# Second attention's beginning: values copied by GpSimd, q's transfers on two queues in both parts, q arranged ahead, second x turned a job later

## The reference, cut to what matters

```python
def _L1_attn_ref(x, Wq, bq, Wk, bk, Wv, bv, Wo, bo):
    # W = 32, H = 16 heads, G = 2 groups of keys and values, D = 16, R = H // G = 8
    q = (xp @ Wq + bq).reshape(B, Lp, H, D).transpose(0, 2, 1, 3)
    k = (xp @ Wk + bk).reshape(B, Lp, G, D).transpose(0, 2, 1, 3)
    v = (xp @ Wv + bv).reshape(B, Lp, G, D).transpose(0, 2, 1, 3)
    starts = jnp.arange(num_windows) * (W // 2)
    idx = starts[:, None] + jnp.arange(W)
    qw, kw, vw = q[:, :, idx, :], k[:, :, idx, :], v[:, :, idx, :]
    qg = qw.reshape(B, R, G, num_windows, W, D)
    scores = jnp.einsum('brgnqd,bgnkd->brgnqk', qg, kw) * scale
    attn = jax.nn.softmax(scores, axis=-1)
    og = jnp.einsum('brgnqk,bgnkd->brgnqd', attn, vw)
    o = og.reshape(B, H, num_windows, W, D).transpose(0, 2, 3, 1, 4).reshape(B, num_windows * W, H * D)
    return o[:, :L, :] @ Wo + bo
```

## Time and profile before

| | |
|---|---|
| median of 3 runs | 1158.51 us (1154.85 to 1162.67) |
| the profiled execution's own time | 1155.04 us |
| its span in the trace | 1153.2 us |
| TensorE busy | 1114.8 us, 97% of the span |
| VectorE busy | 743.3 us, 64% |
| ScalarE busy | 525.1 us, 46% |
| GpSimd busy | 252.7 us, 22% |

### The profile page before, as it was taken

How to read it: one execution, slowest core, us unless ns; L and a number is a source line. 1 busy time by engine, 2 the same in 40 slices (tenths; PEclk the granted TensorE clock), 3 DMA queues, 4 the chain that set the end, 5 groups by cost and what they waited for, 6 DMA issues and landing times. The chain is left out here.

```text
span 1153.2 us, 20280 instructions
## 1 busy us (share of the span) xinstructions
PE 1114.8 (97%) x7188; PEld 960.1 (83%) x7188; DVE 743.3 (64%) x1582; ACT 525.1 (46%) x978; POOL 252.7 (22%) x290
## 2 busy tenths in 40 slices
PE   8999999999999999999999999899998889899997
PEld 7997988989989989988988888775555778788897
DVE  6665665665665665665665677755554767686556
ACT  5675344344344344344344354555552466644322
POOL 1112021021021021111111131323332556323211
PEclk9999999999999999999999999799998969999999
DMA  4001001001001001001000000853333324000001
GB/s 156 11 1 37 11 1 38 9 0 36 9 0 36 9 0 36 9 0 36 9 0 1 1 1 4 318 123 97 98 102 96 87 77 147 1 1 1 19 19 38
DMA packets 27979, 48.28 MB, mean 42 GB/s; under 512 B 4780, under 2 KB 18060, under 8 KB 26764
## 3 DMA queue, kind: packets, MB, share of 16 engines
q1 hardware_dynamic: 23980, 37.62, 10.2%
q0 software_dynamic: 3456, 9.44, 3.1%
q10 hardware_dynamic: 480, 0.40, 0.1%
HBM read 35.65 MB, written 9.44 MB: 39 GB/s over the span
## 5 line engine op out<-in xcount | busy, mean ns | idle before, releaser
L880 POOL TENSOR_TENSOR linear_out_row<-linear_out_row,lin_sq 128x512 f32<-128x512 f32 x62 | 89.9, 1450 | 538.3 <-ACT lin_sq L745 536.0
L43 PE MATMUL lin_bank<-keep_xT_hi,lin_w_hi 128*128 128x512 f32 x382 | 154.2, 404 | 0.0
L44 PE MATMUL lin_bank<-keep_xT_lo,lin_w_hi 128*128 128x512 f32 x382 | 151.1, 395 | 0.0
L45 PE MATMUL lin_bank<-keep_xT_hi,lin_w_lo 128*128 128x512 f32 x382 | 150.8, 395 | 0.0
L825 DVE TENSOR_TENSOR lin_st<-lin_bank,lin_mask 128x512 f32<-128x512 f32 x64 | 44.0, 691 | 160.9 <-PE lin_bank L622 160.9
L741 ACT ACTIVATE lin_o<-lin_bank 128x512 f32<-128x512 f32 x64 | 38.3, 599 | 187.7 <-PE lin_bank L653 187.7
L649 PE MATMUL lin_bank<-lin_st,lin_v 128*128 128x128 f32 x512 | 93.8, 275 | 0.0
L653 PE MATMUL lin_bank<-lin_qd,lin_state 128*128 128x128 f32 x448 | 87.2, 276 | 0.0
L45 PEld LDWEIGHTS lin_bank<-keep_xT_hi,lin_w_lo 128*128 128x128 f32 x382 | 71.8, 188 | 17.5
L44 PEld LDWEIGHTS lin_bank<-keep_xT_lo,lin_w_hi 128*128 128x128 f32 x382 | 72.0, 189 | 14.6
L43 PEld LDWEIGHTS lin_bank<-keep_xT_hi,lin_w_hi 128*128 128x128 f32 x382 | 72.0, 188 | 14.6
(11 more groups left out here) (417 smaller groups left out, 2843.2 us busy)
## 6 DMA issues: line engine op xcount, KB each, us to landing
lin_raw<-in_wp SPq DMA_DIRECT2D x7, 1024.0 KB, 4.7
experts_up_expert_up<-in_wgu SPq DMA_DIRECT2D x16, 352.0 KB, 7.3
sorted_y<-shared_loaded SPq DMA_DIRECT2D x40, 128.0 KB, 1.7
linear_out_row<-in_wdn SPq DMA_DIRECT2D x4, 704.0 KB
lin_raw_out<-in_wop SPq DMA_DIRECT2D x8, 256.0 KB, 2.6
tokens_x<-linear_out_row SPq DMA_DIRECT2D x4, 512.0 KB, 10.3
linear_out_row<-in_ffn_up SPq DMA_DIRECT2D x2, 1024.0 KB, 5.8
tail_q<-tail_qT SPq DMA_DIRECT2D x28, 64.0 KB, 2.0
```

The costliest lines, as they stand in the source:

```text
L43: nc.tensor.matmul(out, lh, rh, start=first, stop=False, skip_group_check=skip)
L44: nc.tensor.matmul(out, lh, rl, start=False, stop=False, skip_group_check=skip)
L45: return nc.tensor.matmul(out, ll, rh, start=False, stop=last, skip_group_check=skip)
L880: pool.tensor_tensor(part, part, sq[:, a, :], ALU.add).then_inc(squares_sb, 1)
```

## The change

Five things are changed in `window_attention`:

1. `duplicate(0)` leaves ScalarE. GpSimd does its four copies (L2526 of the changed kernel), after the gathers of the two groups `used` and ahead of b's two `pool_scale`; ahead of the copies it waits until the gathers of the last three tiles have landed, and behind them until the copies are done. TensorE's `turn_v` waits for the new count.
2. q's transfers of part (0, 1) are shared like those of (0, 0): four on SyncE, four on ScalarE. Batch 1's stay on SyncE.
3. `arrange(0, 1)` is taken from VectorE (job 0's place) and `arrange(1, 1)` from ScalarE's loop (i = 2); both are done by ScalarE ahead of the loop, behind `arrange(1, 0)`.
4. ScalarE loads its table of the exponential ahead of `arrange(0, 0)` instead of behind it.
5. TensorE turns b's x at i = 2 instead of i = 1.

```diff
--- before.py
+++ after.py
@@ -2496,13 +2496,13 @@
                             at = b * 2 * GD + half * GD + g * WD
                             sp.dma_start(k2[at:at + WD, half, g, :], kvT[g * WD:(g + 1) * WD, b, half * STEP:half * STEP + WPAIRS * WIN]).then_inc(k_moved[b], DMA)
                     for rr in range(RR):
-                        move_q(sp, b, rr, (0, 1) if b == rr == 0 else range(4))
+                        move_q(sp, b, rr, range(4) if b else (0, 1))
                 sp.wait_ge(taken, TT)
                 for n in range(BATCH * RR):
                     sp.wait_ge(q_moved[n], 8 * DMA)
                 for b in range(BATCH):
                     sp.wait_ge(k_moved[b], 4 * DMA)
-                sp.wait_ge(vdup_sb, BATCH)
+                sp.wait_ge(vdup_sb, 2 * WG + 1)
                 fetched.load(sp, w["ffn_up"], w["ffn_down"])
 
             @block.gpsimd
@@ -2517,6 +2517,14 @@
                 (a, b), (c0, c1) = used, rest
                 for n, t in enumerate(ORDER):
                     if n == BATCH * USED_TILES:
+                        for t_ahead in ORDER[n - AHEAD:n]:
+                            pool.wait_ge(arrived[t_ahead], 2 * DMA)
+                        pool.wait_ge(kv_sb, 2)
+                        for half in range(2):
+                            v = kvT[GD:2 * GD, 0, half * STEP:half * STEP + WPAIRS * WIN].rearrange("p (m k) -> p m k", k=WIN)
+                            for g in range(WG):
+                                pool.tensor_copy(vdup[GD:2 * GD, :, half, g, :], v).then_inc(vdup_sb, 1)
+                        pool.wait_ge(vdup_sb, 2 * WG)
                         b.pool_scale(pool, chain, "y")
                         b.pool_scale(pool, chain, "x")
                     if n >= RING:
@@ -2613,8 +2621,6 @@
                         dve.wait_ge(before.added, 1)
                         for half in range(2):
                             turn.statistics(dve, chain, 0, half)
-                    if i == 0:
-                        arrange(0, 1)
                     if i == 2:
                         b.dve_low(dve, turned)
                         b.dve_low_tail(dve, tail_bank[1])
@@ -2672,8 +2678,7 @@
 
                 def duplicate(b):
                     act.wait_ge(kv_sb, 2 * b + 2)
-                    if b:
-                        act.wait_ge(v_mm, b)
+                    act.wait_ge(v_mm, b)
                     for half in range(2):
                         v = kvT[GD:2 * GD, b, half * STEP:half * STEP + WPAIRS * WIN].rearrange("p (m k) -> p m k", k=WIN)
                         for g in range(WG):
@@ -2712,12 +2717,14 @@
                 take_q(0, 0)
                 move_q(act, 0, 0, (2, 3))
                 take_q(0, 1)
-                duplicate(0)
-                arrange(0, 0)
+                move_q(act, 0, 1, (2, 3))
                 act.wait_ge(powered, 1)
                 act.activation(table[:], power[:, 0:1], ACT.Exp)
+                arrange(0, 0)
                 values(0)
-                arrange(1, 0)
+                for part in range(2):
+                    arrange(1, part)
+                arrange(0, 1)
                 for i in range(NJ + 4):
                     if i == 1:
                         act.wait_ge(a.turned, KT + 1)
@@ -2738,8 +2745,6 @@
                         if i >= 2:
                             act.wait_ge(t_mm, i - 1)
                         act.activation(prob[i % 2], less[i % 2], ACT.Exp, scale=float(WD) ** -0.5).then_inc(prob_sb, 1)
-                    if i == 2:
-                        arrange(1, 1)
                     if 2 <= i < NJ + 2:
                         n = i - 2
                         act.wait_ge(t_mm, n + 1)
@@ -2803,7 +2808,7 @@
                         project(q_bank[b][n], wq_hi, wq_lo, slice(rr * P, (rr + 1) * P), b, n).then_inc(q_mm, 1)
 
                 def turn_v(b):
-                    pe.wait_ge(vdup_sb, b + 1)
+                    pe.wait_ge(vdup_sb, 2 * WG + b)
                     if b:
                         pe.wait_ge(q_sb, 2 * BATCH * RR)
                     for m in range(WPAIRS):
@@ -2862,7 +2867,7 @@
                             last = pe.matmul(bank[4][:, j * VS:(j + 1) * VS], pT[n % 2][:, j * P:(j + 1) * P], v2[:, b, mq * 4 + j, :],
                                              start=True, stop=True)
                         last.then_inc(o_mm, 1)
-                    if i == 1:
+                    if i == 2:
                         pe.wait_ge(used[0].low, KT + 1)
                         used[1].pe_turn(pe, turned)
                         pe.wait_ge(v_sb, 1)
```

## The result

The changed kernel takes 1166.7 us (median of 8 runs, 1161.3 to 1170.8) against 1160.0 for the kernel before in the same measurement: a ratio of 1.0066, 95% interval 1.0047 to 1.0086. It is slower by 0.7%, 10 us over the forecast of 1156.5. Its eight times fall into two groups, four from 1161.3 to 1164.6 us and four from 1168.9 to 1170.8, with the median between them; the trace (1161.6) is of the lower group, and no trace of the upper one was caught. On another chip the changed kernel took 1153.1 us against 1153.8, and there the forecast's sign was right.

What follows compares the result with a forecast made beforehand. Before batch 1's keys and values, TensorE was taken to wait on ScalarE's and VectorE/GpSimd's chains; afterwards its own time bounds. Path -0.2 and clock -1.7 us gave about -2: 1156.5 us against 1158.51, range 1150.5 to 1163.

Steps and rivals of the forecast that it cites:

- The step that failed: From batch 1's keys and values at 943.35 us TensorE has hardly a gap, so earlier gains or losses reach the end.
- the last sign of being wrong: A new gap on TensorE behind 946 us that gives the gain back; listed as a sign, with no size.
- the sum: Path to batch 1's projection -0.2 us plus clock -1.7: -1.9, about -2 us; median 1156.5 us.
- the range: Whole kernel time from 1150.5 to 1163 us: cases from 1153 to 1161, widened by some 2 to 3 each side.
- GpSimd's copies: Four copies of the values on GpSimd from 917.6 us, 1.2 us each, with ends of 0.31 and 1.86.
- The exclusion: GpSimd's copies and VectorE's weighing of b's tiles shut each other out, making VectorE's chain 4.0 us later.
- my 931.8: VectorE's start on job 0, forecast at 927.78 + 4.0 = 931.8 us; a sign of being right.
- Its chain: ScalarE's q transfers, table and arranges ahead of the loop, with the last arrange ending at 931.0 us.
- my first rival: ScalarE becomes the bound, job 2's scores start with the last arrange at 931.0: some -4 to -5, 1154 us; chance 0.2.
- The clock term: TensorE, without a gap from 933.2 us, runs product and projection at the high level: -1.7 us, ends 0 and about -3.
- The late gathers: GpSimd's twelve gathers for the last tiles start 4 us later, land before VectorE wants them, and cost nothing.

Runs made afterwards that it cites:

- h1: The changed kernel, nothing edited, timed again on a further chip: 1162.5 us, ratio 1.0047 to the kernel before.
- e1: The changed kernel with duplicate(0) back on ScalarE, so GpSimd copies nothing: 1161.4 us, ratio 1.0036 to the kernel before.
- e2: The changed kernel with b's x turned at i = 1 again: 1159.3 us, ratio 1.0014 to the kernel before.
- h3: The changed kernel with batch 1's first pair of gathers issued between GpSimd's two products of the up stage: 1157.7 us, ratio 0.9988 to the kernel before.
- h4: The changed kernel with each of the six late gather pairs held until VectorE has made a job's differences: 1157.9 us, ratio 0.9990 to the kernel before.
- j1: The changed kernel a third time, beside the kernel before on a further chip, with a trace: 1153.1 us, ratio 0.9990.
- e4: The kernel before with b's x turned at i = 2 as the only change: 1159.6 us, ratio 1.0004 to the kernel before.
- g1: The kernel before without its last twelve gathers (batch 1's): 1155.6 us, ratio 0.9982 to the kernel before.
- g4: The kernel before with late gather pairs, the first apart, each waiting for one more job's differences on VectorE: 1157.4 us, ratio 1.0000.
- h2: The kernel before with four GpSimd copies into unread rows as a delay ahead of the late gathers: 1157.3 us, ratio 0.9995 to the kernel before.
- e3: The changed kernel with q's transfers, the table and all arranges as before, keeping GpSimd's copies and the later turn: 1161.8 us, ratio 1.0019 to the kernel before.
- g3: The changed kernel with late gather pairs, the first apart, each waiting for one more job's differences on VectorE: 1155.2 us, ratio 0.9981 to the kernel before.
- g2: The changed kernel without its last twelve gathers (batch 1's): 1152.6 us, ratio 0.9960 to the kernel before.
- i1: The changed kernel again, unedited, for a trace on a chip not used so far: its single execution or i2's took 1151.1 us, the other 1151.4.
- i2: The changed kernel once more, unedited, for a second trace on the same chip as i1: the two single executions took 1151.1 and 1151.4 us.
- j2: The kernel before, unedited, submitted as a kernel of its own for a second trace beside j1: 1154.5 us, ratio 1.0003.
- i4: The changed kernel with batch 1's first gather pair between GpSimd's two products and the last four pairs paced: 1153.4 us, ratio 0.9995 to the kernel before.

## Why the prediction was wrong

- **The step that failed:** "from there on the engine has hardly a gap, so what is won or lost ahead of it goes through to the end". That was read from one execution of before, in which no release came late, and it is false twice. Where releases are late, the stretch behind 943.35 is no fixed 17.5 us: it was 22.7, 23.4, 23.5 and 21.2 in after, h1, e1 and e2, of which TensorE was idle for 2.4, 4.5, 4.6 and 2.7 and ran the rest at 0.78 to 0.89 of its clock. Where they are not, 4.1 us of what is won come back behind 954, as lower clock and one more gap. The nearest to it in the prediction is the last sign of being wrong, "a new gap behind 946 us that gives the gain back"; no rival had it, and it had no price. The up stage, on which the sum puts nothing, was 3.2 us longer too.
- **How far this is shown.** The traces are of the lower group of after's times. That the late releases turn the sign there rests on h3 and h4 beside h1 and on the traces without them. What lifts the median out of the range is the upper group, and of that no trace exists.
- **What the late releases add up to.** After's first trace against j1's, stretch by stretch: 33.83 - 30.79 = 3.0, 28.47 - 24.50 = 4.0, 22.69 - 15.71 = 7.0, and 4.7 less in the last: 9.3 us, with the lower clock that comes with them. The kernel before is slower on the same chips as well (medians 1158 to 1160 against 1154 on the last two), by some 4 to 6 us, where after is by some 9 to 14, the upper group included. Four near relatives of before (e4, g1, g4 and h2) have the late release of the up stage, so it probably pays there too; its own slower executions have no trace.
- **GpSimd's copies.** I took 1.2 us each and asked for 1.0 to 1.4. They took 2.69 / 4 = 0.67 (j1: 2.95 / 4 = 0.74, from 918.51 on, 0.9 later than forecast), and one with no weighing beside it 0.61. I had doubled the row of 622 ns for 256 elements because these have 512; a copy of 32 partitions by 512 costs about what that row costs undoubled. The Trainium skill's 769 ns for 512 elements (GPSIMD Engine Reference, section 3.1), which I set beside the sum, was the nearer figure.
- **The exclusion.** The mechanism was right and its price was not: I charged VectorE 4.0 us. In j1, whose batch 0 starts within 0.3 us of the trace of before, job 0's reduction starts at 928.65 against 927.78: 0.6 after that offset.

```profile
919.08 0.79 POOL L2526 COPY tail_oP<-linear_out_row 32x512 f32<-32x512 f32 x1
919.43 0.71 DVE L2577 SCALAR_TENSOR_TENSOR keep_y<-linear_out_row,keep_weight,keep_y 128x256 f32<-128x256 f32 x1
...
920.57 0.90 POOL L2526 COPY tail_oP<-linear_out_row 32x512 f32<-32x512 f32 x1
921.03 0.71 DVE L2577 SCALAR_TENSOR_TENSOR keep_y<-linear_out_row,keep_weight,keep_y 128x256 f32<-128x256 f32 x1
...
928.65 0.68 DVE L2613 TENSOR_REDUCE tail_most<-tail_bank 128x16 f32<-128x512 f32 x1
```

  The Trainium skill (SBUF — State Buffer, section SBUF: two separate sides) has the two engines exclude each other for a whole instruction. The rows agree. The copy ends at 919.87 and the weighing that began within it 0.28 us later; the next pair ends at 921.46 and again 0.28 later. In all 14 traces with such copies each weighing of 0.71 us beside them ends 0.27 to 0.28 us behind a copy, and each copy of 0.79 to 0.90 us ends 0.46 to 0.47 behind a weighing. But a turn is cheap: a weighing is issued while the copy still runs and so loses 0.23 us, not the copy's whole time, and the statistics between them lose nothing. I had added four whole copies of 1.2 us. In after's first trace job 0 stands at 931.82, my 931.8 to the digit, and that is luck: there q was turned late. ScalarE got its second half at 920.71, 5.1 us behind the projection instead of 3.3, though its last product had ended at 918.64 + 0.28 = 918.92, so this was one more late release, of 1.8 us:

```profile
918.64 0.28 PE L45 MATMUL tail_bank<-keep_xT_hi,window_wq_lo 128*128 128x264 f32 x1
```

- **ScalarE.** Its chain was right. The last arrange was forecast for 931.0 and ended at 927.38 + 3.38 = 930.76 in j1, where job 2's scores wait for it. That is my first rival, "ScalarE becomes the bound" (0.2 of the chance), in the stretch ahead of the projection, and its 1154 us are near j1's 1153.1:

```profile
926.03 4.10 PE L2846 MATMUL tail_bank<-linear_out_row,tail_q 64*128 64x128 f32 x16 [2.54 <-issue]
930.81 2.07 PE L2846 MATMUL tail_bank<-linear_out_row,tail_q 64*128 64x128 f32 x8 [0.68 <-ACT tail_q L2698]
...
933.73 1.70 PE L2355 MATMUL tail_bank<-keep_ident,window_turn_z 128*128 128x128 f32 x8
935.36 0.29 PE L2363 MATMUL tail_bank<-keep_ident,window_before_z 16*128 16x16 f32 x2
935.58 1.16 PE L2846 MATMUL tail_bank<-linear_out_row,tail_q 64*128 64x128 f32 x8
...
938.50 0.37 PE L2793 MATMUL tail_bank<-keep_xT_hi,window_wkv_hi 128*128 128x264 f32 x1
```

- **The clock term** of -1.7 (0 to -3) was near its far end where nothing was held: job 3's scores take 1.16 us instead of 2.07 and the product follows at the higher level too. In after's first trace it gave nothing; the granted clock was 0.63 from 945 to 948 us, where before had 0.93.
- **The late gathers.** I wrote that they "cost nothing, but have 2 us of cover only", and looked at the one who waits for their rows. Where they cost anything, it came through those who wait for TensorE while they run.
- **The range** rested on three runs of before and took the spread of the times as noise. The chips and hours differ by more than these three runs did: 1154 to 1160 us for the kernel before, and 1153 to 1167 for the changed one.

## What to carry to other kernels

Before a gap is priced, look at what else is in flight where the work lands: a stretch "without a gap" in one trace is one execution, and a second trace of the same kernel, from another chip if possible, is worth more than a finer sum. Waits marked "remote", or a consumer that starts us after both its inputs are complete, are a release that came late; test it by taking away or pacing the indirect transfers beside it, before blaming the edit. Split every longer stretch into idle time and clock before a cause is named: e3's was clock alone. And ask of every gain at the lower clock what the engine will get behind it: 4 of 7 us went back, 2.7 of them as clock. Last, where the times of a kernel fall into two groups, a trace of one group does not explain a median between them.

## What the runs showed of the hardware

- TensorE's semaphore increments can come through late while GpSimd's indirect gathers stream. In after the last packets of a burst moved at 899.2 and 949.1 and the consumer started at 900.19 and 949.91; in e1 948.6 and 949.40, in e2 949.2 and 949.95, in e3 949.6 and 950.24, in e4 946.8 and 947.30. It isn't strict: in h1 one late release (945.16) came 2.0 us before the stream's end, in h2 1.2, in h3 2.6 (942.98) and 0.4, and in g3 0.4 before it. The late release of the up stage stands in after's trace and in all twelve of e1 to h4 (ScalarE idle for 4.8 to 6.6 us ahead of it), and in neither trace of before. It costs what waits behind it: the stretch takes 33.8 us in after and 30.9 in g4, against 30.6 in before. Behind batch 1's projection it went when the late gathers did (g1, g2) or were spread (g4, h4).
- The gathers are not enough for it: i1, i2, j1 and j2 had the same streams and no late release. Two chips were without it, at least three with it; they also were used at different times, so chip and hour are not told apart. Whether TensorE's increments wait in the chip or are only seen late by the others was not tested apart; the consumers did start late, and in after, e1, e2, h1 and h3 TensorE itself halted within a group of products or transposes, for 0.3 to 1.2 us at a time. No trace without late releases has such a halt.
- A paced or earlier gather won 4.6 to 4.9 us over the same kernel on a chip with late releases (h3 and h4 against h1) and nothing where there are none (i4). No version beat the kernel before beyond the interval on its chip, except g1 and g2, which leave work out, and by 0.7 us the changed kernel itself in j1 (0.9990, at most 0.9999).
- VectorE's weighing (two operands in SBUF) and GpSimd's copy shut each other out: a weighing begun within a copy ended 0.28 us behind it, a copy begun within a weighing 0.47 behind it, where they take 0.47 and 0.61 us alone.
- The same 134 matmuls behind batch 1's projection took 15.7 us at a granted clock of 1.00 (j1), 17.5 at 0.89 (before) and 20.8 at 0.73 (e3), all three without idle time.
